# Attention denominators in a fused FFN-attention-FFN kernel: adding up exponentials by DMA and by GpSimd in two buffers

## The reference

```python
x = x + 0.5 * ffn(layernorm(x))      # 8 experts, top 2, silu(x w1) * (x w2) times w3
x = x + attn(layernorm(x))           # the block that the change touches
x = x + 0.5 * ffn(layernorm(x))
# attn: 16 query heads of 32, 4 key/value heads, rope, causal mask over t = 2048
attn = einsum('bhqd,bhkd->bhqk', q, k) / sqrt(32)
attn = softmax(where(mask, -inf, attn))     # exp(s - max) / sum over keys
out  = einsum('bhqk,bhkd->bhqd', attn, v);  return out @ wo
```

## Time and profile before

| | before |
|---|---|
| median of 3 runs | 1362.54 us |
| profiled execution | 1354.8 us, span 1353.5 us |
| TensorE busy | 1218.2 us (90%) |
| VectorE busy | 883.8 us (65%) |
| ScalarE busy | 662.0 us (49%) |
| GpSimd busy | 612.6 us (45%) |
| attention, first to last exponential | 436.5 to 1079.4 us |
| groups 8 to 15 | about 636 to 1082 us |

### The profile page before, as it was taken

The page is one execution under the profiler, slowest core; times in us unless marked ns, Lnnn a source line. Parts: engine busy times, 40 slices in busy tenths (PEclk is TensorE's granted clock), DMA queues, the critical chain, the costliest instruction groups (busy, mean ns, idle before and its releaser), DMA issues.

```text
span 1353.5 us, 22135 instructions
## 1 busy us (share of the span) xinstructions
PE 1218.2 (90%) x7484; PEld 781.8 (58%) x7484; DVE 883.8 (65%) x2058; ACT 662.0 (49%) x1313; POOL 612.6 (45%) x497
## 2 busy tenths in 40 slices
PE   5499999859888999999999999999999966999996
PEld 4478888637776554445445455445443335777774
DVE  7867777578996665566576666587660066666664
ACT  2545555435455554354365555356566651444442
POOL 5644444223210111012425634436384691888886
PEclk9789999979999999999999999999999987999998
DMA  9823333256550032034004202013200054566665
GB/s 335 322 87 110 109 110 109 82 160 110 83 84 28 7 66 32 1 96 63 1 33 95 33 1 96 31 46 82 33 1 1 1 198 155 94 100 104 100 105 78
DMA packets 62508, 114.43 MB, mean 85 GB/s; under 512 B 8288, under 2 KB 27744, under 8 KB 62368
## 3 DMA queue, kind: packets, MB, share of 16 engines
q0 software_dynamic: 31728, 68.17, 23.9%
q1 hardware_dynamic: 30672, 44.85, 9.8%
HBM read 79.71 MB, written 33.55 MB: 84 GB/s over the span
## 4 chain that ended last, share of the span: by engine, by line
PE 62%; DVE 15%; DMA 11%; issue 5%; ACT 4%; POOL 3%; SPq 1%; POOLq 0%; DVEq 0%; ACTq 0%
PE bank L823 10%; PE bank L1521 10%; PE bank L1533 10%; PE bank L980 8%; PE bank L846 5%; PE bank L1546 5%; PE bank L1583 3%; DMA out<-Y,DI 3%; DVE PM L993 3%; DMA XG<-xn,TK 3%; POOL out L773 3%; DMA XA<-y 2%; PE bank L805 2%; DVE bank L995 2%; ACT P L1625 1%
## 5 line engine op out<-in xcount | busy, mean ns | idle before, releaser
L1625 ACT ACTIVATE P<-bank 128x512 f32<-128x512 f32 (+3 forms) x640 | 305.5, 536 | 296.6 <-PE bank L1521 292.8
L993 DVE TENSOR_REDUCE PM<-bank 128x1 f32<-128x512 f32 x384 | 252.8, 685 | 99.4 <-PE bank L980 98.3
L1521 PE MATMUL bank<-Qs,Ks 98*128 98x512 f32 (+3 forms) x640 | 248.0, 412 | 7.9 <-ACT P L1625 6.3
L980 PE MATMUL bank<-Ks,Qs 96*128 96x512 f32 (+3 forms) x640 | 238.5, 391 | 8.3 <-DVE PM L993 5.2
L1521 PEld LDWEIGHTS bank<-Qs,Ks 98*128 98x128 f32 x640 | 117.2, 190 | 149.8 <-issue 84.7
L1679 POOL TENSOR_TENSOR CH<-CH,P 128x512 f32<-128x512 f32 x128 | 160.3, 1285 | 70.4 <-ACT P L1625 69.5
L1664 POOL TENSOR_SCALAR_AFFINE_SELECT P<-P 128x512 f32<-128x512 f32 x64 | 40.9, 639 | 308.4 <-ACT P L1625 308.4
L995 DVE CUSTOM_DVE_ANT_0 bank<-bank,KB 128x128 f32<-128x128 f32 (+3 forms) x256 | 124.8, 497 | 57.6 <-PE bank L980 56.9
L980 PEld LDWEIGHTS bank<-Ks,Qs 96*128 96x128 f32 x640 | 121.4, 190 | 62.6 <-DVE PM L993 32.6
L1533 PE MATMUL bank<-P,V 128*32 128x512 f32 (+3 forms) x1280 | 150.8, 542 | 0.2 <-POOL P L1664 0.2
L773 POOL DMA_INDIRECT out<-Y,DI x78 | 126.3, 1619 | 40.0 <-issue 30.6
(11 more groups left out here) (186 smaller groups left out, 1920.3 us busy)
## 6 DMA issues: line engine op xcount, KB each, us to landing
xn<-XN SPq DMA_DIRECT2D x8, 1024.0 KB, 7.1
WR<-L_ffn_w POOLq DMA_DIRECT2D x16, 512.0 KB, 15.5
XO<-y POOLq DMA_DIRECT2D x8, 1024.0 KB, 9.5
WR<-L_ffn_w SPq DMA_DIRECT2D x16, 512.0 KB, 8.3
XA<-y POOLq DMA_DIRECT2D x24, 256.0 KB, 4.2
W<-L_ffn_w POOLq DMA_DIRECT2D x8, 512.0 KB, 24.9
XA<-L_attn_x SPq DMA_DIRECT2D x16, 256.0 KB, 3.6
XO<-L_attn_x SPq DMA_DIRECT2D x4, 1024.0 KB, 7.9
```

The source lines that it names most:

```text
L980: pe.matmul(bk(g, bank)[:, 0:n], g.Qs[b][0:96, G % 4 * 4 + h, c * P:c * P + P], g.Ks[0:96, G % 4, k * BQ:k * BQ + n], start=True, stop=Tru ...
L993: dve.tensor_reduce(dst, bk(g, bank)[:, 0:n], AX.X, ALU.max).then_inc(s(f"free{bank}"), 1)
L1521: pe.matmul(bk(g, i % 3)[:, o:BQ], g.Ks[0:98, G % 4, k * P:k * P + P], g.Qs[G // 4][0:98, G % 4 * 4 + j, o:BQ], start=True, stop=True).the ...
L1625: act.activation(a.P4[buffer_of(n)][:, j, o:BQ], bk(g, i % 3)[:, o:BQ], ACT.Exp, scale=scale).then_inc(s("exp"), 1)
```

## The change

In groups 8 to 15 every third full key tile (`MOVED`: 0, 3, 6 and, with 16 tiles, 9) is no longer read by GpSimd's adds or TensorE's ones-matmuls. SyncE copies the first one by a plain DMA from `P4` into a new buffer `CD`; GpSimd issues DMAs that add the others onto `CD` (`onto`), and, at the first diagonal tile, one that adds `CH` onto `CD` (`MERGED`). Each of these DMAs moves four heads by 512 floats on 128 partitions, 1024 KB. GpSimd's own adds take the other full tiles: `(1, 2, 4, 5, 7)` and `(1, 2, 4, 5, 7, 8, 10)`, as many links as before. TensorE takes `CD` in at the group's end where it took `CH`. There is one `CH` and one `CD` for all groups. TensorE sums only what is left: the four diagonal tiles, and tile 11 in the groups of 16.

```diff
-    a.CH = [big(f"CH{i}", [P, 4, BQ]) for i in range(2)]
+    a.CH = big("CH", [P, 4, BQ])
+    a.CD = big("CD", [P, 4, BQ])
...
-ADDED = ((), (), (0, 1, 3, 4, 6), (0, 1, 3, 4, 6, 7, 9))
+ADDED = ((), (), (1, 2, 4, 5, 7), (1, 2, 4, 5, 7, 8, 10))
+MOVED = ((), (), (0, 3, 6), (0, 3, 6, 9))
+FIRST_SUMS = 8
...
+COPIED = {n: G - FIRST_SUMS for n, (G, k) in enumerate(TILES) if k in MOVED[G // 4][:1]}
+MERGED = [n for n, (G, k) in enumerate(TILES) if MOVED[G // 4] and k == 4 * (G // 4)]
+ONTO = {n: i for i, n in enumerate(n for n, (G, k) in enumerate(TILES) if k in MOVED[G // 4][1:] or n in MERGED)}
...
+        if last and MOVED[b]:                                  # TensorE, weigh
+            pe.wait_ge(s("onto"), 16 * (ONTO[n - k + 4 * b] + 1))
...
+            elif old in COPIED:                                # ScalarE, before it writes P4 again
+                act.wait_ge(s("copied"), 16 * (COPIED[old] + 1))
+            elif old in ONTO:
+                act.wait_ge(s("onto"), 16 * (ONTO[old] + 1))
...
-        if new and G >= 10:                                    # GpSimd, link
-            pool.wait_ge(s("chain"), G - 9)
+        if new and G > FIRST_SUMS:
+            pool.wait_ge(s("onto"), 16 * (ONTO[MERGED[G - FIRST_SUMS - 1]] + 1))
...
+    def onto(n):                                               # GpSimd, after the tile's mask and link
+        G, k = TILES[n]
+        if n in MERGED:
+            pool.wait_ge(s("link"), LINKS[n - k + ADDED[G // 4][-1]] + 1)
+            one = a.CH
+        else:
+            pool.wait_ge(s("exp"), 4 * n + 4)
+            one = a.P4[buffer_of(n)]
+        if k == MOVED[G // 4][1]:
+            pool.wait_ge(s("copied"), 16 * (G - FIRST_SUMS + 1))
+        else:
+            pool.wait_ge(s("onto"), 16 * ONTO[n])
+        pool.dma_start(a.CD[:], one[:], accum_op=ALU.add).then_inc(s("onto"), 16)
...
+    def copied(n):                                             # SyncE
+        G = TILES[n][0]
+        sp.wait_ge(s("exp"), 4 * n + 4)
+        if G > FIRST_SUMS:
+            sp.wait_ge(s("chain"), G - FIRST_SUMS)
+        sp.dma_start(a.CD[:], a.P4[buffer_of(n)][:]).then_inc(s("copied"), 16)
```

More of the change, by code:

```diff
@@ L1385 @@
 MASKED = {n: i for i, n in enumerate(n for n, (G, k) in enumerate(TILES) if k >= G // 4 * 4)}
-ADDED = ((), (), (0, 1, 3, 4, 6), (0, 1, 3, 4, 6, 7, 9))
+ADDED = ((), (), (1, 2, 4, 5, 7), (1, 2, 4, 5, 7, 8, 10))
+MOVED = ((), (), (0, 3, 6), (0, 3, 6, 9))
+FIRST_SUMS = 8
 LINKS = {n: i for i, n in enumerate(n for n, (G, k) in enumerate(TILES) if k in ADDED[G // 4][1:])}
-SUMMED = {n: i for i, n in enumerate(n for n, (G, k) in enumerate(TILES) if k not in ADDED[G // 4])}
+COPIED = {n: G - FIRST_SUMS for n, (G, k) in enumerate(TILES) if k in MOVED[G // 4][:1]}
+MERGED = [n for n, (G, k) in enumerate(TILES) if MOVED[G // 4] and k == 4 * (G // 4)]
+ONTO = {n: i for i, n in enumerate(n for n, (G, k) in enumerate(TILES) if k in MOVED[G // 4][1:] or n in MERGED)}
+SUMMED = {n: i for i, n in enumerate(n for n, (G, k) in enumerate(TILES)
+                                     if k not in ADDED[G // 4] + MOVED[G // 4])}
 def buffer_of(n):
@@ L1535, in weigh @@
         ins.then_inc(s("weigh"), 1)
-        if last and ADDED[b]:
-            pe.wait_ge(s("link"), LINKS[n - k + ADDED[b][-1]] + 1)
+        if last and MOVED[b]:
+            pe.wait_ge(s("onto"), 16 * (ONTO[n - k + 4 * b] + 1))
             for h in range(4):
-                ins = pe.matmul(bk(g, 4)[32 * h:32 * h + 32, :], g.ones[:], a.CH[G % 2][:, h, :], start=False, stop=False)
+                ins = pe.matmul(bk(g, 4)[32 * h:32 * h + 32, :], g.ones[:], a.CD[:, h, :], start=False, stop=False)
             ins.then_inc(s("chain"), 1)
         if n in SUMMED:
-            fresh = k == min(i for i in range(4 * b + 4) if i not in ADDED[b])
+            fresh = k == min(i for i in range(4 * b + 4) if i not in ADDED[b] + MOVED[b])
             if fresh and G:
@@ L1670, in link @@
         new = k == ADDED[b][1]
-        to, one = a.CH[G % 2], a.P4[buffer_of(n)]
+        to, one = a.CH, a.P4[buffer_of(n)]
         two = a.P4[buffer_of(n - k + ADDED[b][0])] if new else to
-        if new and G >= 10:
-            pool.wait_ge(s("chain"), G - 9)
+        if new and G > FIRST_SUMS:
+            pool.wait_ge(s("onto"), 16 * (ONTO[MERGED[G - FIRST_SUMS - 1]] + 1))
         if LINKS[n]:
@@ L1688, in pool_attend @@
                 link(n)
+            if n in ONTO:
+                onto(n)
         elif step[0] == "xoy":
@@ L1787, in sp_attend @@
             sp_found(g, b)
+        elif kind == "score" and step[2] == 3 and b in COPIED:
+            copied(b)
         elif kind == "xo":
```

## The result

The changed kernel takes 1371.62 us (median of 20 runs, 1364.33 to 1380.03) beside 1364.55 for the kernel before (20 runs, 1354.50 to 1369.62). The ratio is 1.0067, 95% interval 1.0048 to 1.0086: slower by about 9 us by the ratio (the medians differ by 7.1), where 9.5 us less were forecast. The profiled execution took 1369.37 us.

What follows compares the result with a forecast made beforehand. TensorE, busy 90% of the span, was taken as the bound. Gain -21.7, waits +7.5, +2, +0.9, +2 gave -9.3, taken as -9.5: 1362.5 - 9.5 = 1353.0 us, range for 8 in 10 from 1340 to 1367.

Steps and rivals of the forecast that it cites:

- TensorE's gain: Ones-matmuls of 28 tiles removed, 0.87 us each, 0.75 beside maxima: 21.7 us gained together.
- The DMAs' price: Time of the added 1024 KB DMAs: additions 8.5 us to landing, copies 4.4 to 7.9, GpSimd held 1.13 an issue.
- L: Time of an adding 1024 KB DMA from SBUF into SBUF, issue to landing: taken as 8.5 us, ends 4.4 and 12.
- the copy: SyncE's plain 1024 KB copy of a group's tile 0: between 4.4 and 7.9 us, landing early enough to be free.
- the walk: Group 15 followed in time at L = 8.5: tiles 7, 10, 13 wait 0.4, 3.4, 2.7 us; 7.5 us of gain gone.
- The walk's step from 1042.68 to 1043.42: Group 15, tile 3: delay from the tile's start to its first head being ready for GpSimd's link, given as 0.78 us.
- 4 forecast: Group 15 ends 4 us later than before instead of 3.5 earlier, through waits for the adding DMAs.
- the 9.3 forecast: Net gain of the whole change, gain less waits: 9.3 us, taken as 9.5.
- Issuing a DMA holds GpSimd 1.13 us: GpSimd's queue: each DMA issue delays its next add 1.13 us, read from 951.70 to 952.83.
- whether it keeps up with TensorE: Groups with maxima: VectorE, needed 34.56 of 50 us, turns some gain into waits; 16.5 us kept for 22 tiles.
- the one that ended slower: Rival, chance 0.17: DMA additions slow, L about 12, landings chained; sum near +25 us, 1387; decides from about L = 10.
- slow GpSimd's adds or TensorE's reading: Failure condition, no size given: prediction fails if the DMAs slow GpSimd's adds or TensorE's reading.

Runs made afterwards that it cites:

- hold gone on both sides: Changed kernel and kernel before, each with the maxima's split made of four one-input VectorE reductions: 0.9878 (again 0.9834) and 0.9960 of the kernel before.
- The version with the cast replaced: Changed kernel with the cast of the negated maxima into M2 replaced by a max-reduction over a length-one axis, subtraction kept: 1363.82 us, ratio 1.0025.
- the same with reductions: Changed kernel with the maxima's high/low split made of four VectorE reductions with one SBUF input each: 1343.71 us, 0.9878; second measurement 1342.20, 0.9834.
- the kernel with 4 KB DMAs: Kernel before plus a plain GpSimd DMA of 8 floats a partition, read by nobody, ahead of every link: 1370.15 us, ratio 1.0067.

## Why the prediction was wrong, step by step

**TensorE's gain: right.** With VectorE's hold gone on both sides, groups 8 to 14 take 374.7 us with the change and 393.2 without: 18.4 us for 24 tiles, 0.77 a tile, where 0.75 and 0.87 were taken. What the DMAs cost in these groups is already taken off, so the gain itself is at least that.

**The DMAs' price: mis-sized, on the safe side.** L was 7.1 in the median, not 8.5; the copy 4.7. The new issues held GpSimd 0.6 us before its next addition, not 1.13. In group 15 ScalarE waited before tiles 7, 10 and 13, as the walk has it. These are its rows for tiles 7, 10, 11 and 13 in the changed kernel:

```profile
1062.16 2.06 ACT L1637 ACTIVATE P<-bank 128x512 f32<-128x512 f32 x4 [1.19 <-DMA CD<-P]
1071.39 2.07 ACT L1637 ACTIVATE P<-bank 128x512 f32<-128x512 f32 x4 [1.95 <-DMA CD<-P]
1074.30 2.08 ACT L1637 ACTIVATE P<-bank 128x512 f32<-128x512 f32 x4 [0.84 <-PE bank L1529]
1083.94 1.64 ACT L1637 ACTIVATE P<-bank 128x384 f32<-128x384 f32 x4 [3.50 <-PE bank L1529]
```

The walk's step from 1042.68 to 1043.42 is 0.74 us and not 0.78, which changes nothing. With the landings of this group (8.6, 6.8 and 6.8 us) and 0.6 us an issue, it gives waits of 0.6, 1.5 and 2.0 us; measured, beyond the 0.55 and 1.34 us that stand before such tiles anyway, are 0.6, 1.4 and 2.2. Group 15 came out 2.6 us longer than before (4 forecast). Part of that is the clock: its mean in the group was 0.89. The version with the cast replaced waited as long before tiles 7 and 10 (1.21 and 1.87 us), ran at 1.00 and took 46.9 instead of 48.7 us. The prediction let a wait cost its own length and did not count what TensorE can lose behind it. With the hold gone on both sides, the change is worth 15.9 us in groups 8 to 15 (439.3 to 423.4), more than the 9.3 forecast.

**The step that failed: "Issuing a DMA holds GpSimd 1.13 us".** The issue was charged to GpSimd's own queue and to nobody else, and for the stretch with maxima the prediction asked of VectorE only whether it keeps up with TensorE. In its place the runs showed that an issue just ahead of a link makes that link hold VectorE's casts, scalings and two-input instructions until its last addition is done. Four casts were caught, each with TensorE stopped behind it (18.5 us together) and slow afterwards: 27.6 us in groups 11 to 14 between the changed kernel and the same with reductions, more than the whole gain. No rival named it; the one that ended slower had another cause, and its condition (L of 10 or more) was not met. The sentence on DMAs that "slow GpSimd's adds or TensorE's reading" came near and looked at the wrong engines.

Could the rows of before have shown it? In part. In the kernel before, a cast beside a link already took 0.44 us and the subtraction 1.22, where they take 0.17 and 0.18 alone: VectorE waits for an addition's end. Here are GpSimd and VectorE of the kernel before in group 12:

```profile
886.36 5.01 POOL L1679 TENSOR_TENSOR CH<-CH,P 128x512 f32<-128x512 f32 x4 [1.95 <-ACT P L1625]
...
889.72 0.44 DVE L1012 CAST M<-NM 128x16 fp32r<-128x16 f32 x1
890.19 1.22 DVE L1014 TENSOR_TENSOR M<-NM,M 128x16 fp32r<-128x16 f32 x1
```

The cast ends at 890.16, inside the link, near the end of its third addition. That a link behind a DMA issue lets nobody in between its additions stands in no row of before, as none of its casts began behind such an issue. That was luck, and close: in group 13 the subtraction ended at 952.00, within the residual's DMA issue, and the link behind it began at 952.83. But a spread from 0.17 to 1.22 us on an instruction of 16 numbers was there to be asked about.

## What to carry to other kernels

Work given to GpSimd has a second price beside its own time: it stopped VectorE's casts, scalings and instructions with two SBUF inputs here, and a DMA issued by GpSimd right ahead of a run of its additions lengthened the stop from one of them to all. Before moving work there, list VectorE's casts, copies, scalings and two-input instructions that fall beside it, look at the spread of their durations and not at the mean, and ask who waits for them; reductions over an axis of length one can stand in for small ones (shown here for 16 numbers a partition only). And price a wait of TensorE's with the slow clock behind it.

## What the runs showed of the hardware that I had not expected

- A cast, a scaling and a subtraction with two SBUF inputs took 1.6 to 6.1 us beside four GpSimd additions that followed a DMA issue. Beside additions that did not, casts took at most 0.95 us, subtractions 1.22, and a scaling that takes 0.54 alone 1.34. A reduction at the same moment took 0.17 to 0.19 us. Almost every long hold ended with the link. The exceptions fit the gaps: in group 8 of the kernel with 4 KB DMAs GpSimd paused 1.4 us inside a link for ScalarE, and a cast of 1.82 us ended there; in group 14 of the changed kernel a second link followed 0.08 us later, where GpSimd waits for its own signal, and the cast ended between the two (1016.02).
- The issue does not hold from its first moment: the subtraction of the kernel before that began 0.13 us into one (951.83 behind 951.70) took 0.18 us; the cast of group 12 in the changed kernel, 0.26 us into one (884.25 behind 883.99), was held.
- What in the issue closes the additions to VectorE stays open. By the records an addition behind an issue starts before the last is over, by 0.25 to 0.72 us in the four links of the changed kernel that held a cast, but by 0.04 to 0.08 in those of the kernel with 4 KB DMAs and by 0.03 to 0.06 in links with no issue ahead, where GpSimd did not wait: the overlap does not tell which link holds. Only that 0.08 us without an addition ends the hold is shown.
- Adding 1024 KB from SBUF onto SBUF takes 7.1 us from issue to landing in the median, adding it from DRAM 9.4 in the same run, a plain copy from SBUF to SBUF 4.7, and a 16 KB addition 2.1. Single additions took 6.8 to 10.3 us, and 13.8 in group 9, where two more DMAs of 1024 KB were issued within 0.4 us.
- Behind an idle stretch of 3.8 us TensorE's granted clock was 1.2 GHz (0.50) for some 7 us (817.4 to 824.3). In the changed kernel the mean clock of groups 11 to 14, with the held casts, was 0.91 to 0.95, and of group 15 0.89, against 1.00 before.
